# A selective-scan kernel: the loop of four engines written out over all 32 chunks

## What is computed

```
dA  = exp(delta[..., None] * A)                      # 1024 channels x 16 states
dBu = (delta * u)[..., None] * B[:, :, None, :]
h   = dA_t * h + dBu_t                               # step by step over time
y_t = einsum('bdn,bn->bd', h, C_t)
```

## Time and profile before

| | |
|---|---|
| median of 3 runs | 7681.41 us |
| profiled execution, first to last instruction | 7682.2 us |
| DVE busy | 7049.2 us (92%) |
| POOL busy | 6971.3 us (91%) |
| PE busy | 6897.7 us (90%) |
| ACT busy | 6115.7 us (80%) |

### The profile page before, as it was taken

The page is one execution under the profiler, slowest core; times in us unless marked ns, Lnnn a source line. Parts: engine busy times, 40 slices in busy tenths (PEclk is TensorE's granted clock), DMA queues, the critical chain, the costliest instruction groups (busy, mean ns, idle before and its releaser), DMA issues. The chain is left out here.

```text
span 7682.2 us, 138746 instructions
## 1 busy us (share of the span) xinstructions
PE 6897.7 (90%) x32682; PEld 4066.2 (53%) x32682; DVE 7049.2 (92%) x10433; ACT 6115.7 (80%) x11545; POOL 6971.3 (91%) x3774
## 2 busy tenths in 40 slices
PE   6899988899898989999898999999888999999889
PEld 3455555555555555555555555555555555555445
DVE  2899999999999999999999999999899999999766
ACT  1788888888788888888788888888888888888745
POOL 0899999999899999999899999999899999999768
PEclk8999999999999999999999999999999999999999
DMA  8444445444444554444445534444454344444555
GB/s 258 144 134 133 127 137 147 130 116 139 128 130 123 148 147 112 134 138 135 122 126 148 148 102 144 131 134 132 124 148 138 108 143 134 134 131 126 150 198 170
DMA packets 605621, 1066.12 MB, mean 139 GB/s; under 512 B 113584, under 2 KB 221872, under 8 KB 596336
## 3 DMA queue, kind: packets, MB, share of 16 engines
q1 hardware_dynamic: 602704, 1055.84, 46.4%
q10 hardware_dynamic: 2080, 1.05, 0.0%
HBM read 926.61 MB, written 130.05 MB: 138 GB/s over the span
## 5 line engine op out<-in xcount | busy, mean ns | idle before, releaser
L692 POOL TENSOR_TENSOR dBu<-Bb,du 128x1024 f32<-128x1024 f32 x2048 | 4790.1, 2365 | 97.1 <-DVE hV L1164 57.3
L808 ACT ACTIVATE scans<-delta,A 128x512 f32<-128x512 f32 x4096 | 2772.7, 693 | 612.9 <-DVE scans L1164 271.6
L1164 DVE TENSOR_TENSOR_SCAN scans<-scans,state,dBu 128x512 f32<-128x512 f32 x2304 | 2907.9, 1282 | 378.5 <-ACT scans L808 321.8
L1018 PE MATMUL yT<-ident,hC 128*128 128x128 f32 x9216 | 1424.5, 284 | 358.8 <-DVE hC L1180 347.0
L1180 DVE TENSOR_TENSOR hC<-scans,Cb 128x512 f32<-128x512 f32 x2304 | 1557.6, 677 | 14.4 <-PE yT L1018 14.1
L701 POOL TENSOR_TENSOR hR<-hR,Cb 128x512 f32<-128x512 f32 x1024 | 1290.8, 1271 | 251.3 <-DVE state L1198 245.6
L1018 PEld LDWEIGHTS yT<-ident,hC 128*128 128x128 f32 x9216 | 1068.2, 144 | 804.5 <-DVE hC L1180 567.4
L1164 DVE TENSOR_TENSOR_SCAN hR<-scans,state,dBu 128x512 f32<-128x512 f32 x1024 | 1290.2, 1260 | 0.8 <-ACT scans L808 0.4
L1011 PE MATMUL bg<-u,comb 128*128 128x512 f32 x2112 | 989.1, 594 | 0.9 <-DVE u L1127 0.9
L1164 DVE TENSOR_TENSOR_SCAN hV<-scans,state,dBu 128x512 f32<-128x512 f32 x768 | 966.7, 1259 | 14.0 <-ACT scans L808 13.8
L950 PE MATMUL bg<-hT,win_u 128*128 128x512 f32 x2112 | 963.9, 597 | 0.9 <-ACT hT L728 0.9
(11 more groups left out here) (165 smaller groups left out, 7652.7 us busy)
## 6 DMA issues: line engine op xcount, KB each, us to landing
comb<-pre_scratch SPq DMA_DIRECT2D x1040, 256.0 KB, 4.6
Bb<-bc_scratch SPq DMA_DIRECT2D x264, 512.0 KB, 8.6
Cb<-bc_scratch SPq DMA_DIRECT2D x264, 512.0 KB, 7.8
win_u<-in_win SPq DMA_DIRECT2D x264, 256.0 KB, 5.0
pre_scratch<-pre SPq DMA_DIRECT2D x264, 256.0 KB, 3.7
comb<-comb_scratch SPq DMA_DIRECT2D x66, 1024.0 KB, 7.2
win_z<-in_win SPq DMA_DIRECT2D x257, 256.0 KB, 2.7
part_scratch<-pre SPq DMA_DIRECT2D x132, 256.0 KB, 2.0
```

Source lines behind the costliest of these rows:

```text
L692: pool.tensor_tensor(dBu[:, q % AHEAD], Bb[:, 2 * q:2 * q + 2, :], du[:, j % 2, :].unsqueeze(1).broadcast_to([P, 2, T]), ALU.mult).then_in ...
L808: act.activation(dA[dA_bank(v, j, n)][:], delta[:, j % 2, :], ACT.Exp, scale=A[:, v % 2, j * N + n:j * N + n + 1]).then_inc(dA_made, 1)
L1018: ins = nc.tensor.matmul(yT[:, tt * P:(tt + 1) * P], product[:, tt * P:(tt + 1) * P], ident[:], start=first and tt == 0, stop=False, is_tr ...
L1164: nc.vector.tensor_tensor_scan(to, dA[dA_bank(v, j, n)][:], dBu[:, q % AHEAD, k, :], state[:, c:c + 1], ALU.mult, ALU.add).then_inc(h_made, 1)
```

## The change

`TURN` and the `Fori` go from the programs of POOL, ACT, PE and DVE. Each now loops over all 32 chunks in Python, so the code is written out four times as long, and i, g and all values waited for are constants. The order of the instructions is the same. Conditions that asked whether c or g is a register now ask whether it is over 0. `dA_bank` takes i in place of v: the bank is (n + i * 8 + j) % 3, so that the three banks go on turning past the eighth chunk. SP's loops stay. The rest of the diff is indentation.

```diff
-TURN = 8
...
-        dA_bank = lambda v, j, n: (n + v * MT + j) % 3
+        dA_bank = lambda i, j, n: (n + i * MT + j) % 3
...
-            with pool.Fori(0, CHUNKS // TURN) as r:
-                for v in range(TURN):
-                    i, s = r * TURN + v, v % 2
-                    for j in range(MT):
-                        g = i * MT + j
...
+            for i in range(CHUNKS):
+                s = i % 2
+                for j in range(MT):
+                    g = i * MT + j
...
-                if not isinstance(g, int) or g > 0:
+                if g > 0:
                     act.wait_ge(delta_made, g)
...
-                if m < 2 and not isinstance(c, int):
+                if m < 2 and c > 0:
                     act.wait_ge(out_stored[m], c * 32 + O0)
...
-                    act.wait_ge(A_loaded[s], r * (8 * TURN) + (v // 2 * 16 + 16))
+                act.wait_ge(A_loaded[s], i // 2 * 16 + 16)
```

More of the change, by code:

```diff
@@ L807, in step_dA @@
                         act.wait_ge(h_made, g * N - N + before + 1 + H0)
[L808 to L809 removed]
+                act.activation(dA[dA_bank(i, j, n)][:], delta[:, j % 2, :], ACT.Exp,
+                               scale=A[:, i % 2, j * N + n:j * N + n + 1]).then_inc(dA_made, 1)
             nc.scalar.preload_act_table_set(EXP_LN)
@@ L845, in _ @@
             act.wait_ge(bg_free, PRO)
[L846 to L850, removed]
-                    act.wait_ge(A_loaded[s], r * (8 * TURN) + (v // 2 * 16 + 16))
[L852 to L893, removed]
-                                if kind == "C":
[L895 to L911, removed]
-                                for kind, m in GATED[p]:
-                                    if kind == "C":
-                                        silu_u(freed(i, f"C{m + 1}"), m, 2, 1 - s)
-                                    else:
-                                        silu_z(freed(i, f"Z{m}"))
-                                nc.scalar.preload_act_table_set(EXP_LN)
@@ L946, in project_u @@
                 pe.wait_ge(wu_loaded[m % RING], (c * per + m // RING + 1) * 16)
-                if m == 0 and not isinstance(c, int):
+                if m == 0 and c > 0:
                     pe.wait_ge(bg_free, freed(c - 2, "H3"))
@@ new lines, in _ @@
+            for i in range(CHUNKS):
+                s = i % 2
+                for j in range(MT):
+                    g = i * MT + j
+                    dve.wait_ge(state_kept, g - 6 + K0)
+                    for q in range(NQ):
+                        p = j * NQ + q
+                        dve.wait_ge(state_saved, kept(g, q) + S0)
+                        dve.wait_ge(dBu_made, g * NQ + q + 1)
+                        for k in range(2):
+                            n = 2 * q + k
+                            c = j * N + n
+                            dve.wait_ge(dA_made, g * N + n + 1 + DU0)
+                            if n in ASIDE:
+                                dve.wait_ge(hR_used, aside(g, n) + 1)
+                                to = hR[:, ASIDE.index(n), :]
+                            elif n in TURNED:
+                                dve.wait_ge(bg_ready, ready(i if j else i - 1, f"T{((j - 1) % MT) * N + n}"))
+                                dve.wait_ge(turned_saved, g + V0)
+                                to = hV[:, TURNED.index(n), :]
+                            elif n in IN_PLACE:
+                                to = dA[dA_bank(i, j, n)][:]
+                            else:
+                                h_free(g, n)
+                                to = h[:]
+                            nc.vector.tensor_tensor_scan(to, dA[dA_bank(i, j, n)][:], dBu[:, q % AHEAD, k, :],
+                                                         state[:, c:c + 1], ALU.mult, ALU.add).then_inc(h_made, 1)
+                        if q == 1:
+                            name = f"Y{(j - 1) % MT}"
+                            gate(ready(i, name), bg[OWN_BANK], g - 1, (j - 1) % MT, s if j else 1 - s)
+                        pair = (2 * q, 2 * q + 1)
+                        own = [n for n in pair if n in STRAIGHT]
+                        for n in own:
+                            c = j * N + n
+                            dve.wait_ge(h_made, g * N + n + 1 + H0)
+                            bank = dA[dA_bank(i, j, n)] if n in IN_PLACE else h
+                            if len(own) == 1:
+                                nc.vector.tensor_copy(state[:, c:c + 1], bank[:, T - 1:T]).then_inc(state_saved, 1)
+                            dve.wait_ge(hC_used, straight(g, n) - C0 + 1)
+                            if j == 0 and n == own[0]:
+                                dve.wait_ge(C_loaded[q], i * 16 + 16)
+                            nc.vector.tensor_tensor(hC[:, (j * NS + STRAIGHT.index(n)) % HC, :], bank[:],
+                                                    Cb[:, n, :], ALU.mult).then_inc(hC_made, 1)
+                            if n == pair[0]:
+                                dve.wait_ge(h_made, g * N + n + 2 + H0)
+                            if n == pair[0] and len(own) == 2:
+                                if dA_bank(i, j, n + 1) == 0:
+                                    nc.vector.tensor_copy(state[:, c:c + 2], scans[:, 0:2, T - 1]).then_inc(state_saved, 1)
+                                else:
+                                    nc.vector.tensor_copy(state[:, c:c + 1], h[:, T - 1:T])
+                                    nc.vector.tensor_copy(state[:, c + 1:c + 2],
+                                                          dA[dA_bank(i, j, n + 1)][:, T - 1:T]).then_inc(state_saved, 1)
+                        for n in pair:
+                            for ns, places, saved in [(ns, hR, aside_saved) for ns in COPIES] + [(TURNED, hV, turned_saved)]:
+                                if n != ns[-1]:
+                                    continue
+                                dve.wait_ge(h_made, g * N + n + 1 + H0)
+                                k = (ASIDE if places is hR else TURNED).index(ns[0])
+                                step = ns[1] - ns[0] if len(ns) > 1 else 1
+                                nc.vector.tensor_copy(state[:, j * N + ns[0]:j * N + n + 1:step],
+                                                      places[:, k:k + len(ns), T - 1]).then_inc(saved, 1)
```

191 lines of the change are left out of this document (110 added, 81 removed).

## The result

| | before | after |
|---|---|---|
| median | 7678.85 us (4 runs) | 7778.49 us (4 runs, 7778.0 to 7795.3) |
| profiled execution | 7682.2 us | 7793.5 us |
| hV state copies held by POOL | 106 of 256 | 251 of 256 |
| state copy from hV, in all | 126.4 us | 298.0 us |
| executed instructions | 138746 | 111380 |

The change makes the kernel slower: ratio 1.0132, 95% interval 1.0118 to 1.0147, which is +100 us. The forecast was 7730, +48 us. "Held" is said here of a copy from hV that took over 0.3 us, where one that runs freely takes 0.16.

The account below looks back on a forecast made before the run. DVE was taken to set the pace, with ACT delaying it in places and POOL having slack. The terms -30 + 78 + 11 - 3 - 8 = +48 us on 7682 gave 7730 us, range 7645 to 7790.

Parts of the forecast that it names:

- The sign and its mechanism: Main forecast: slower, 7700 to 7770 us, chance 0.58, as constants move DVE's last-ending hC_made wait ahead of its scan.
- 850 places: h-writing scans on DVE left to pay 0.10 us each for the moved wait: +85 us, +78 after absorption.
- a fourth place: Scan 10, counted among four places a tile hanging on hC_made, except behind held hV copies in 106 tiles.
- The edges: Three loop branches, each leaving DVE idle about 10 us for "issue"; straight code removes them: -30 us.
- The held copies: hV state copies on DVE, some 85 us of holding in 106 tiles; delays at scan 8 fall into it: -7 us.
- the prediction's own signs of being wrong: Scans 2, 8 and 12 still at 0.72 us, new issue gaps, or hV copies held other than 106 of 256.
- ACT, PE and POOL: Constants save ACT and PE register instructions; DVE sees it only where ACT is late: -8 us, bounds 0 and -25.
- Late dA at scan 0: 110 scans 0 waiting for ACT's dA get two sequencer instructions behind its release: +11 us, bounds -10 and +20.
- slower by more: Rival, chance 0.1: hV copies meet POOL's products more often, another 60 held copies, +50 us, 7780 us.
- Register instructions: Removing them on DVE gains nothing, except behind late releases: -3 us at scans into hV that wait for dA.
- Code supply: Instruction fetch for the written-out code: nothing put against it, with an upper bound of 30 us.

Follow-up runs that it names:

- experiment 2: Changed kernel with the hC_made wait listed first on DVE for every scan that writes h, and a spare wait left out: 7604.48 us, ratio 0.9906.
- experiments 3 and 4: State copies from hR and hV one column at a time: 3 in the changed kernel, 7637.77 us; 4 with hC_made also listed first, 7569.67 us.
- experiment 1: Kernel before with 16 chunks a turn in place of 8 on all four engines, register waits kept: 7659.94 us, ratio 0.998.
- experiment 8: Changed kernel with DVE alone looped, eight chunks a turn with register waits; PE, ACT and POOL written out with constants: 7662.77 us, ratio 0.9976.

## Why the prediction was right in direction and short in size

**The sign and its mechanism: right.** hC_made moved into the sequencer instruction ahead, its price is 0.10 us (0.716 to 0.816, 0.713 to 0.818, 0.715 to 0.809 at scans 2, 8 and 12), scans 4 and 14 kept 0.597, no "issue" gap is left, and experiment 2 takes all of the loss away by the order of the waits alone. The prediction had 850 places at this price, less 7 us absorbed: +78. Scans 2, 8 and 12 gave +76, experiments 3 and 4 differ by 70. Scan 10, counted as a fourth place in part, has no price of its own to be seen, as in nearly every tile the held copy is what it starts after.

**The edges: right.** -30 forecast, 28 by the tiles around them, 18 for two of the three in experiment 1. The Trainium skill, Runtime: NRT & Kernel Launch, section Instruction fetch mechanics, has the rule for it, a branch outside the window stalls and straight code does not; the trace agrees with it, 9.9 to 10.2 us a branch in experiment 8 and no gap in the straight code.

**The held copies: the step that failed.** The sum kept the holding at 106 of 256 tiles and took 7 us off for a delay absorbed in it; that it could grow was a rival with 0.1, priced at 60 more copies and 50 us. It grew by 145 copies and 171 us (86.0 to 257.3 us over the copy's own time). Another rate than 106 of 256 stood among the prediction's own signs of being wrong, and it came. About half of the holding reaches the end: undoing scan 8's delay alone gives 123 us back, of which 26 are its own price and 97 the holding's, while the copies became 190 us shorter (298.0 to 108.0). On the 171 us that the change added this is some 87, an estimate to within some 15. The rest had replaced other waits. DVE's waits for ACT at scan 10 fell from 82 to 44 us, and those at scan 0 from 108 times (the prediction counted 110) to 62. The prediction had all it needed to see this, copies from 0.154 to 1.32 us long, and did not ask what decides between the two: it put the chance of a hold at a rate, where it is a race with a margin. In the timelines above the margin is 0.01 to 0.02 us (the copy at 6.21, POOL's product at 6.22 and 6.23); the shift was 0.10.

**Without the extra holding the sum would have been too high.** The changed kernel less those 87 us is 7691, +13 us and not +48. Two terms were off. *ACT, PE and POOL:* -8 forecast, about -18 by experiment 8 (10 to 28 by its interval), near the far one of the bounds given. *Late dA at scan 0:* +11 forecast. The price was right (+0.108 us), but not the count: a slower DVE finds ACT in time more often, so 62 tiles pay it, and beside the edges the tile's end became 50 us shorter. In experiment 2, with DVE fast again, ACT is late at scan 0 in 124 tiles. The two-column copy from hR, not in the sum, gave another 15. So the 52 us between forecast and result are two errors of opposite sign: a gain of some 35 us overlooked, a loss of some 87 us left to a rival. That the time lies in the stated range, 12 us below its upper end, is in part luck: the prediction's sum with the loss alone would be about 7817. It is luck too that the rival "slower by more" named 7780, since it had 60 more held copies and not 145.

**Register instructions: right at nothing.** 27366 fewer executed instructions, and the only places on DVE that I found shorter by them are those behind a late release, as forecast: at scan 9, where dA_made is listed first, a late scan now starts 0.034 us after ACT and not 0.189, which with fewer such waits (34 to 16) gave 6.8 us, and not 3.

**Code supply: right at nothing.** The instruction queues moved 7.2 MB against 9.2, and experiment 2's straight code has no gap.

## What to carry to other kernels

Turning register waits into constants changes which wait rides on the instruction: list the one that is met last first, and look at each op again that starts right behind its releaser. Where a short op is sometimes long, find the op of the other engine that it races, the point at which both engines were last in step, and the margin between them; a delay counts only between these two. Price a delay by undoing it at one place at a time, since equal delays of 0.10 us were worth 23, 33 and 123 us here, of which the first two can't be told apart and the third stands clear.

## What the runs showed of the hardware that I had not expected

A DVE copy of three columns, 0.16 us long, waits for the end of a product that POOL has already begun, in all up to 1.27 us in the changed kernel, while DVE's scans and hC products beside the same POOL products keep their length (scans 1.283 us on the mean in both kernels). Copies of one column were never held (1792 in experiment 3, none over 0.149 us), nor were two-column copies from PSUM, where those of two columns from hR took up to 0.59 us before. The Trainium skill, SBUF — State Buffer, section SBUF: two separate sides, describes this as an exclusive lock on a port pair that VectorE and GpSimd share, for the whole instruction, taken on VectorE's side by ops in a two-port mode; the trace agrees, with ends 22 to 32 ns behind POOL's. VectorE: DVE Perf Modes of the Trainium skill, section Mode 2×_2P — use both read ports for one tensor, asks for a single source in SBUF and an outer dimension that is even, or odd and equal on both sides. Three columns to three meet that, a PSUM source does not, and the runs agree: two-column copies from PSUM took at most 0.16 us, beside POOL's products too. A copy of one column has no such dimension, and none was held. What no run here tested is a three-column copy out of PSUM.

The three engines' edges overlap without adding up: 31 us with DVE's branches alone, 18 with those of the other three alone, 28 with all.
